# A fused attention and feed-forward kernel: the last batch's rows stored unnormalized and normalized by GpSimd after the gather

## What is computed

```python
def _layernorm(x, axis=-1, eps=1e-05):
    m = jnp.mean(x, axis=axis, keepdims=True)
    v = jnp.var(x, axis=axis, keepdims=True)
    return (x - m) / jnp.sqrt(v + eps)
...
    x = x + _L0_xattn_ref(_layernorm(x, axis=-1), ctx_4096, ctx_4096, ...)
    x = x + _L0_ffn_ref(_layernorm(x, axis=-1), L0_ffn_up, L0_ffn_down, L0_ffn_perm)
```

## Time and profile before

| | us |
|---|---|
| median of 3 runs | 1519.7 |
| lowest and highest | 1517.99, 1523.19 |
| span of the profiled execution | 1516.6 |
| PE busy in that span | 1496.1 (99%) |
| DVE busy | 1192.4 (79%) |
| ACT busy | 1065.8 (70%) |
| POOL busy | 962.8 (63%) |

### The profile page before, as it was taken

One profiled execution on the slowest core, in us unless ns is written; L12 is line 12 of the kernel. 1 busy time (PEld: TensorE's weight loads), 2 busy tenths in 40 slices (PEclk: granted clock), 3 DMA queues, 4 the chain that ended last, 5 costly groups with the idle time before them and its releaser, 6 DMA issues.

```text
span 1516.6 us, 19144 instructions
## 1 busy us (share of the span) xinstructions
PE 1496.1 (99%) x6592; PEld 1233.7 (81%) x6592; DVE 1192.4 (79%) x1514; ACT 1065.8 (70%) x1321; POOL 962.8 (63%) x765
## 2 busy tenths in 40 slices
PE   8999999998999999999999999999999999999998
PEld 7878888887888888888888888888888888777886
DVE  4989868875788767887678877888778876889876
ACT  4636757844878568784687847878378773899876
POOL 1673686297862668626784357834579355898887
PEclk9999999999999999999999999999999999999999
DMA  9998788786677936778376784767747776768886
GB/s 327 330 379 332 229 301 298 269 265 204 202 264 266 276 118 221 246 262 278 119 237 248 246 260 133 261 237 250 231 146 275 249 237 204 236 197 257 289 285 221
DMA packets 166865, 374.76 MB, mean 247 GB/s; under 512 B 14960, under 2 KB 80496, under 8 KB 158576
## 3 DMA queue, kind: packets, MB, share of 16 engines
q1 hardware_dynamic: 141424, 281.25, 56.3%
q0 software_dynamic: 25344, 92.29, 17.3%
HBM read 287.45 MB, written 86.03 MB: 246 GB/s over the span
## 4 chain that ended last, share of the span: by engine, by line
PE 80%; DVE 4%; POOL 4%; DMA 4%; ACT 3%; issue 3%; SPq 0%; POOLq 0%; ACTq 0%; DVEq 0%
PE PP L892 13%; PE PP L938 12%; PE PP L953 12%; PE PP L896 6%; PE PP L941 6%; PE PP L957 6%; PE PP L879 6%; PE PP L880 6%; PE PP L874 6%; PE PP L909 4%; PE PP L913 2%; POOL out L1346 1%; POOL FB L1338 1%; POOL FB L1341 1%; ACT Z L1031 1%
## 5 line engine op out<-in xcount | busy, mean ns | idle before, releaser
L938 PE MATMUL PP<-GG,WW 128*128 128x512 f32 x1008 | 270.5, 390 | 4.4 <-issue 4.4
L1046 ACT ACTIVATE PP<-PP 128x1024 f32<-128x1024 f32 x256 | 262.0, 1024 | 0.0
L1249 DVE TENSOR_TENSOR R<-PP,R 128x1024 fp32r<-128x1024 f32 x175 | 213.6, 1220 | 52.5 <-ACT PP L1046 50.6
L892 PE MATMUL PP<-R,WC 128*128 128x512 f32 x1024 | 253.1, 389 | 0.7 <-ACT Z L998 0.7
L1330 POOL TENSOR_TENSOR X<-X,RAW 128x512 f32<-128x512 f32 x112 | 189.2, 1725 | 96.4 <-DVE bn L1069 71.6
L1045 ACT ACTIVATE R<-PP 128x1024 fp32r<-128x1024 f32 x175 | 180.1, 1029 | 87.5 <-PE PP L941 86.5
L938 PEld LDWEIGHTS PP<-GG,WW 128*128 128x128 f32 x1008 | 189.6, 188 | 44.4 <-issue 4.8
L892 PEld LDWEIGHTS PP<-R,WC 128*128 128x128 f32 x1024 | 192.1, 188 | 41.0 <-ACT Z L998 1.1
L1084 DVE TENSOR_TENSOR R<-RAW,R 128x1024 fp32r<-128x1024 f32 x128 | 184.1, 1445 | 49.8 <-ACT R L976 49.8
L1346 POOL DMA_INDIRECT out<-FB,perm_sb x128 | 153.4, 1198 | 82.0 <-DVE FB L1255 64.1
L1323 POOL DMA_INDIRECT FB<-xg_scratch,perm_sb x128 | 127.7, 997 | 115.1 <-DMA xg_scratch<-FB 74.4
(11 more groups left out here) (122 smaller groups left out, 2582.5 us busy)
## 6 DMA issues: line engine op xcount, KB each, us to landing
WW<-w_scratch SPq DMA_DIRECT2D x148, 512.0 KB
X<-in_x SPq DMA_DIRECT2D x32, 1024.0 KB, 6.0
RAW<-in_cx SPq DMA_DIRECT2D x32, 1024.0 KB
RAW<-in_xT SPq DMA_DIRECT2D x63, 512.0 KB
RAW<-in_cT SPq DMA_DIRECT2D x63, 512.0 KB
xg_scratch<-FB SPq DMA_DIRECT2D x104, 256.0 KB
w_scratch<-WW POOLq DMA_DIRECT2D x16, 1024.0 KB, 6.8
HX<-wp_scratch SPq DMA_DIRECT2D x7, 1024.0 KB, 8.2
```

The source lines that it names most:

```text
L892: eng.matmul(PP[2 + ot // 2][:, ot % 2, :], WC[:, l, ct, part(ot)], u[:, ct, :], start=(l == 0 and ct == 0), stop=False)
L938: eng.matmul(pp[:, e, :], wt[:, l, part(2 * p + e)], g[:, 0, :], start=(l == 0), stop=False)
L1046: eng.activation(pp[:], pp[:], ACT.Gelu).then_inc(S["gelu"], 1)
L1249: eng.tensor_tensor(h_tile(f, p, 1), PP[slot["up", f, p]][:], f32(h_tile(f, p, 0)), ALU.subtract).then_inc(S["hlo"], 1)
```

## The change

Only batch 7 is treated differently. Its rows are stored as they are after the group norm, without `xln2`, so the transposes wait for `x1_piece` alone; they and the eight `x1_piece` steps get new due times: first the left halves of all four channel tiles, their quarter turned and stored, then the right halves. The eight `square_x1` steps are due 3.5 units apart instead of 2. After the last of them, `root_last` takes one power instead of two, and `scale_rows`, `turn_rows`, `store_rows` and `spread_rows` make and broadcast three rows instead of two: r, -m r, and a bias. The broadcast goes to one buffer of `RAW`; a second becomes four slots for normalized tiles. For each of the 16 blocks of batch 7, GpSimd multiplies and adds once the tile is gathered (`norm_row`, due at `lead - 4.45`) and writes the normalized tile to a slot, from which cast and rest are taken; `resid` is gone there, and VectorE adds the bias to the gathered tile (`bias_row`, due at `lead - 1.2`).

```diff
+    def root_last(i):
+        for k in range(2):
+            n.up("rs2", i, k)
...
+    def spread_rows(i):
+        for what in ("nb", "norm"):
+            slot[what] = ring("raw", NRAW)
+            free[what] = take(("raw", slot[what]))
+        n.dma("nbl", i)
...
+    def norm_row(f, k):
+        slot["norm", f] = k
+        free["nrm", f] = take(("NORM", k)) if ("NORM", k) in held else free["norm"]
+        n.up("nmul", f)
+        n.up("nadd", f)
...
         for k in range(8):
-            ct, hf = k // 2, k % 2
-            t = f0 + 5 + 0.8 * k if first else f0 + 3.25 + 2 * (k + 2) if last else base[i + 1] - 0.3 + 0.95 * k
+            ct, hf = (k % 4, k // 4) if last else (k // 2, k % 2)
+            t = f0 + 5 + 0.8 * k if first else f0 + (6.25, 18.25)[hf] + 2 * ct if last else base[i + 1] - 0.3 + 0.95 * k
             put(t, x1_piece, i, ct, hf)
-            put(t + (1.2 if last else 0.9), square_x1, i, ct, hf)
+            put(f0 + 8.45 + 3.5 * k if last else t + 0.9, square_x1, i, ct, hf)
...
-        e = f0 + 12 if first else f0 + 22.8 if last else base[i + 1] + 8.6
+        e = f0 + 12 if first else f0 + 34 if last else base[i + 1] + 8.6
         put(e, sum_sq, i)
...
+        if last:
+            put(e + 0.1, root_last, i)
+            put(e + 1.9, scale_rows, i)
+            put(e + 2.4, turn_rows, i)
+            put(e + 2.5, store_rows, i)
+            put(e + 5, spread_rows, i)
...
-            t = base[i + 1] + TURN[i][q] if not last else e + (6.2, 8.9, 12.1, 14.7)[q]
+            t = f0 + (14.25, 26.25, 30.25, 34.25)[q] if last else base[i + 1] + TURN[i][q]
             for ct in range(NT):
-                put(t + (0.6 if last else 0.25) * ct, turn, i, q, ct)
-            put(t + 3 if last else base[i + 1] + 28.3 if q == NQ - 1 else t + 1.3, store_x, i, q)
+                put(t + (1.0 if last else 0.25) * ct, turn, i, q, ct)
+            put(t + 3.9 if last else base[i + 1] + 28.3 if q == NQ - 1 else t + 1.3, store_x, i, q)
...
-            put(lead - 2.05, resid, f, b)
+            if b == B - 1:
+                put(lead - 4.45, norm_row, f, g % 4)
+                put(lead - 1.2, bias_row, f)
+            else:
+                put(lead - 2.05, resid, f, b)
...
-                act.wait_ge(*at["g", f])
+                act.wait_ge(*(at["nadd", f] if b == B - 1 else at["g", f]))
...
+            elif stage == "scale_rows":
...
+                dve.wait_ge(*at["rs2", i, 1])
+                eng.tensor_copy(cold[:, 0:NT], rs[:, 1, :]).then_inc(S["rowk"], 1)
+                dve.wait_ge(*at["nm1", i, 1])
+                eng.tensor_tensor(cold[:, NT:2 * NT], nm1[:, 1, :], rs[:, 1, :], ALU.mult).then_inc(S["rowk"], 1)
...
-                dve.wait_ge(*(at["xln2", i, ct] if i < B - 1 else at["xln2", i, ct, q // 2]))
+                dve.wait_ge(*(at["xln2", i, ct] if i < B - 1 else at["x1", i, ct, q // 2]))
...
+            elif stage == "bias_row":
+                f = a[0]
+                dve.wait_ge(*at["nmul", f])
+                dve.wait_ge(*at["nbl", B - 1])
+                rows = FB[:, f % NFB, :].rearrange("p (r c) -> p r c", r=4)
+                eng.tensor_tensor(rows, rows, scale_part(2), ALU.add).then_inc(S["rbc"], 1)
...
+            elif stage == "norm_row":
+                f = a[0]
+                pool.wait_ge(*at["g", f])
+                pool.wait_ge(*at["nbl", B - 1])
...
+                eng.tensor_tensor(norm, rows, scale_part(0), ALU.mult).then_inc(S["nmul"], 1)
+                pool.wait_ge(*at["nmul", f])
+                eng.tensor_tensor(norm, norm, scale_part(1), ALU.add).then_inc(S["nadd"], 1)
```

More of the change, by code:

```diff
@@ L336, in x1_piece @@
         t = n.up("x1", i, ct, hf)
-        give(t, ("X", ct))
+        if i < B - 1:
+            give(t, ("X", ct))
         if (ct, hf) == (NT - 1, 1):
@@ L385, in spread_sd, with xln2 @@
         order.append(("spread_sd", i))
-    def xln2(i, ct, half=None):
-        t = n.up("xln2", i, ct) if half is None else n.up("xln2", i, ct, half)
-        if ct == NT - 1 and half != 0:
+    def xln2(i, ct):
+        t = n.up("xln2", i, ct)
+        if ct == NT - 1:
             give(t, ("nm2",))
-        order.append(("xln2", i, ct, half))
+        order.append(("xln2", i, ct))
     def turn(i, q, ct):
@@ L1025, in scalar @@
             elif stage == "xln2":
[L1026 to L1027 removed]
+                i, ct = a
                 act.wait_ge(*at["rs2", i, 1])
```

95 lines of the change are left out of this document (79 added, 16 removed).

## The result

The changed kernel takes 1523.17 us in the median of 22 runs (1519.7 to 1528.55), the kernel before 1519.05 us in 22 runs on the same chip (1513.31 to 1528.01). The ratio is 1.0026, 95% interval [1.0014, 1.0038]: slower by some 4 us, where I had forecast no change. The time lies inside the range of the prediction, but the difference is clear of the noise, and its direction is the one I had given 23%. The profiled execution has a span of 1525.0 us against 1516.6 before.

The account below looks back on a forecast made before the run. PE, busy 99% of the span, bounds the kernel, with GpSimd as good as full in the last stage. Terms -0.9 and +0.9 sum to 0: span 1516.6, median 3.1 above, so 1519.7 us; range 1516.0 to 1525.5.

Parts of the forecast that it names:

- ScalarE's relief: Last stage: eight xln2, 10.0 us of ScalarE, go; of 2.72 us of PE gaps 1.7 are won.
- the 14 steps that the prediction counts: PE's half-block steps between 1357 and 1398 us: they lose 1 us instead of 2.7.
- The two-pair round: GpSimd's round with two multiply-add pairs, before block 26's gather: every later gather comes 2.86 us later.
- The broadcast: Three rows for two, 7.4 us, some 5 us of cover before block 24's multiply; rival that it comes late: 0.06.
- VectorE is not the bound: Rival for batch 7's blocks: g_lo and bias_row both drawn out, 5.9 us against 5.44, 0 to +8 us; chance 0.20.
- -0.9 us up to block 25 and +0.9 behind it: Last stage: 0.9 us gained before block 25 and 0.9 lost behind it, sum 0.
- GpSimd before block 24: Ahead of block 24's gather: a power, the stores' wait and 2 us of scatters saved, so it goes out at 1406.7.
- the wait on the stores: GpSimd's 3.15 us wait at block 24's gather for batch 7's stores goes, except the usual 0.30.
- the credit of 5.85 us: GpSimd's savings before block 24's gather: power 1.0, scatters 2.0, wait on the stores 2.85 us.
- when a cast is ready: Block 25: cast behind norm_row behind the gather, begins at 1423.5, up-matmul at 1425.1; ScalarE's gain falls to 0.9 us.
- The term behind block 25: Blocks 25 to 39: GpSimd rounds of 5.60 against 5.44 lose 2.2 us, less 1.3 for the last round: 0.9.
- 1.0 us for the wait on the power: VectorE's queue at scale_rows, awaiting GpSimd's power: 1.0 of the 2.72 us of PE gaps stays.

Follow-up runs that it names:

- e2: The changed kernel without the residual pair (multiply and add on GpSimd) of block 23; 1521.95 us, ratio 1.0013.
- e6: The changed kernel with root_last ahead of the residual pair of block 19 on GpSimd; 1525.13 us, ratio 1.0038.
- e7: The changed kernel with norm_row's add on VectorE (due 3.3 before the block) and root_last ahead of the residual pair; 1531.67 us, ratio 1.0063.
- e10: The changed kernel with norm_row's add on VectorE behind add_r (due 2.6 before the block) and root_last early; 1543.2 us, ratio 1.0156.
- e12: Like e10, with the last batch's g_lo behind a further h_lo (due 1.7 before the block, not 2.1); 1551.66 us, ratio 1.0209.
- e13: The changed kernel with norm_row's add left out and root_last ahead of the residual pair; 1519.41 us, ratio 0.9989.
- e1: The changed kernel with scale_rows and the transpose behind it due 1.5 units later; 1525.45 us, ratio 1.0029.
- e3: The changed kernel without the bias addition (bias_row) on VectorE in the 16 blocks of batch 7; 1521.83 us, ratio 1.0015.
- e11: The changed kernel with norm_row's add left out altogether, so the cast takes the product; 1519.98 us, ratio 0.9992.
- e5: The changed kernel with norm_row's add moved from GpSimd to VectorE, due 3.3 before the block; 1525.53 us, ratio 1.0033.

## Why the prediction was wrong

**What held.** ScalarE's relief and GpSimd as the engine that is full were read rightly: of the 14 steps that the prediction counts (half blocks 26 to 40) the first ten lose nothing now. But the 14 as a whole lose 4.85 us and not 1, since the wait for the power falls into the last of them. The two-pair round was priced at 2.86 us more; it is 8.08 against the 5.14 of e2, 2.94, and e2 shows that PE pays it. The late rounds were taken as 5.6 us; they are 5.50, three 6.1 to 6.6, and 5.70 in the mean. The broadcast was in time. (The 5.1 us of gaps before were read from waits; by the starts they are 6.2, which changes no term.) VectorE is not the bound: `bias_row` averages 866 ns and not 1.2 to 1.6 us, and `g_lo` 723.

**The sum against the trace.** The prediction had -0.9 us up to block 25 and +0.9 behind it. Measured are +4.05 and +3.78.

**The step that failed first: GpSimd before block 24.** I let the gather of block 24 go out at 1406.7; it went at 1412.24. Of the 2.0 us that the scatters beside the `x1_piece` operations were to give, 0.6 came by block 14. The groups of the stretch 1305 to 1357, after, answer to the earlier trace rows:

```profile
L1445 POOL TENSOR_TENSOR FB<-FB,SMM 128x512 f32<-128x512 f32 x9 | 16.2, 1798 | 0.7
...
L1268 DVE SCALAR_TENSOR_TENSOR Z<-Z,sm,X 128x1024 f32<-128x1024 f32 x7 | 14.1, 2015 | 0.0
L1442 POOL TENSOR_TENSOR FB<-FB,SMM 128x512 f32<-128x512 f32 x9 | 11.8, 1310 | 0.2
L1427 POOL DMA_INDIRECT FB<-xg_scratch,perm_sb x9 | 10.5, 1165 | 2.7 <-issue 1.5 <-DVE GG L1324 1.2
L1450 POOL DMA_INDIRECT out<-FB,perm_sb x9 | 9.8, 1093 | 1.4 <-issue 1.1
```

And the add and the gather of the kernel before in the same stretch:

```profile
L1341 POOL TENSOR_TENSOR FB<-FB,SMM 128x512 f32<-128x512 f32 x9 | 11.6, 1294 | 0.7
L1323 POOL DMA_INDIRECT FB<-xg_scratch,perm_sb x9 | 8.7, 971 | 2.7 <-issue 2.7
```

Nine scatters fell from 1733 to 1093 ns, as I had said, 5.8 us together. But the add grew from 1294 to 1798 ns, 4.5 us, and the gather from 971 to 1165, 1.7 us: the sum of GpSimd's three rows is 0.5 us more than it was. In order of time, four adds beside a piece take 2.16 or 2.17 us and two gathers beside one 1.97 and 1.73; three adds of 1.63 or 1.64 us, each beside a `g_lo` and no piece, make 1.0 of the 4.5. The other two pieces began within 0.05 us of a scatter (1346.36 and 1346.41; 1358.21 and 1358.18), and the scatters took 1.02 us: these cost GpSimd nothing. I had seen that a piece meets another operation if it is moved off the scatter, and had still taken 2 us as won. The next error was the wait on the stores, which I took as 2.85 us won. That wait had hidden another: the gather needs a row buffer whose scatter has landed, and with the stores out of the way GpSimd waited 1.66 us for that at block 24 (and 1.01 at block 19; before, 0.83 more than the usual gap at block 22). Counted from the start of the stage, the credit of 5.85 us was worth 0.81 at block 24's gather.

**The step that failed second: when a cast is ready.** I had the new chain, cast behind `norm_row` behind the next gather, but reckoned that of ScalarE's gain 0.9 us would be left at block 25. With the gathers 5 us later than I thought, the round that `norm_row` asks for was not there: the way from gather to matmul is at least 11.11 us from block 27 on, against 7.6 to 8.8, and at block 27 PE paid the difference of 3.0 us in full.

**The term behind block 25 was too small.** I had +0.9 us for it, with 4.2 as its end. From half block 53 on the loss is 3.96 us, 3.2 more than before: the rounds are 5.70 us in the mean and not 5.60, and the 1.3 us that I took off for the last round, which has no gather, did not come: the step to block 39 loses 0.74 us.

**The step that was mis-sized: 1.0 us for the wait on the power.** It cost 2.29 us and 1.9 more, some 1.5 of them by the clock of 0.66 behind it. In four other executions with the same instructions, in which the clock stayed, the stretch lost 1.4 to 2.5 us. With the power early (e6, e7, e10, e12, e13) half blocks 38 to 41 lose 0.3 to 0.8 us. But e1 and e6 show that the time doesn't follow: with that wait gone, the casts behind it wait for their gathers, and PE for a weight tile. Behind half block 47 the loss is 7.8 us after, 8.2 with `scale_rows` later (e1), 8.5 with the power early (e6), 4.6 without `bias_row` (e3), 4.6 without the pair (e2), 1.9 without the add (e11; 4.4 in e13, the execution far over its median), and 1.2 before; what lightens GpSimd's load lowers it, and what moves the power doesn't.

**What caused it, then.** Shown: GpSimd's one add per block, left out, is worth the loss of time (e11). That run shortens the way to the cast as well as GpSimd's work and doesn't part the two; e2 and e3 speak for the work, since a pair that no cast waits for, and 0.3 us of an add, give 3.2 us each behind half block 47. Shown: a second pair in one round reaches PE nearly whole (e2), and `bias_row` costs by lengthening GpSimd's add (e3). The ratios of these two, 1.0013 and 1.0015, lie at half of after's excess, but their intervals are too wide to divide it. Left open: what the new due times of pieces, squares and stores cost by themselves between half blocks 34 and 47, where every version of the change loses 1.7 to 4.9 us and the kernel before 0.9, since no run has them alone; and a placing of the add on VectorE that closes no ring. No version that computes all of it beats the kernel before; the lowest median among them is that of the changed kernel itself, with e1, e5 and e6 inside each other's intervals.

## What to carry to other kernels

An engine whose round is as long as the bound's is a second bound: what it is relieved of must be followed to the gather or store that then becomes the last to arrive, and a wait that goes should be counted only down to the next wait behind it. When a step is put between a load and its use, count the time from the load's issue to the use before and after, and ask whether the issuing queue has that much in hand; here 3 us more were asked for and none were there. Before an operation is moved to an idle engine, walk once around the queues: if what it waits for, and what waits for it, stand in the same two or three in-order queues, the length of that ring is the new round, however idle the engines are.
